# Tiles of a shared batch between the next batch's halves, gathers in front of scatters, and another order in the routing

## The chip, the cores and the metric

The kernel runs on one core of a Trainium2 chip. The metric is the device time of one execution in microseconds; the median of three runs stands for the kernel. Engines are TensorE (PE), VectorE (DVE), ScalarE (ACT), GpSimd (POOL) and SyncE (SP). SP issues the plain loads and stores, GpSimd the gathers and scatters by index; all of them run on the core's 16 DMA engines.

## The reference

Four batches of 512 tokens with 512 features pass through an attention layer and a mixture of experts, each with a residual:

```python
x = x + xattn(layernorm(x), ctx, ctx)   # keys and values: the context and the tokens, 1024 in all
x = x + ffn(layernorm(x))
# ffn, T = 2048 tokens, E = 64 experts, K = 6, CAP = 128, I = 192, SI = 384
scores = softmax(xf @ gate_w.T);  topk_w, topk_idx = top_k(scores, K)
# every expert takes its first 128 tokens in token order
gu = gx @ gate_up_proj[e];  hid = silu(gu[:, :I]) * gu[:, I:]
eo = (hid @ down_proj[e]) * buf_w            # scatter-added to the tokens
shared = (silu(xf @ shared_gate_w.T) * (xf @ shared_up_w.T)) @ shared_down_w.T
```

All is in float32. The kernel splits every operand of a product into a high and a low part and makes three matmuls of each product (high by high, high by low, low by high).

## The kernel before, in words

**First part.** A loop over the four batches does the attention and the router. The last batch (b = 3) has a body of its own, `last_routes` in the three engines' programs: the choice of experts of its tokens is not scattered to the table in HBM as for the other batches but added up with matmuls. TensorE makes the logits, then positions (`pos`), then a table of token numbers (`tab`) and one of weights (`tabw`); VectorE makes what they need (the one-hot rows `hot`, `chosen_b`, `at_slot` or `slots_hot`, `hot_w`). `idx_ready` is incremented when the rows to gather are known, `kept.routed` when the weights are too. Between these pieces lie pieces of the second part, called through `two.`.

**Second part.** Two kinds of work run together. (1) The experts, one a step: SP loads 2 x 384 KB of gate and up weights and 256 + 128 KB of down weights into rings of three raw buffers (`gu_raw`, `dn_raw`); ScalarE copies the high part (`act_weights`), VectorE subtracts the low part (`dve_weights`); GpSimd gathers 128 rows (256 KB, `gather`), TensorE transposes them (`rows`), multiplies with gate and up (`gate_up`, 12 matmuls of 384 columns), transposes the hidden tile and multiplies with down (`down`, 5 matmuls of 512 columns); ScalarE scales by the weight (`out_rows`, four buffers `eo`), and GpSimd scatters with add (`add_rows`, 256 KB). In step e TensorE does down(e), transpose_hidden(e + 1), gate_up(e + 2), rows(e + 4) and then a piece of the shared work. In step e VectorE makes the splits of experts e + 3 and e + 4; SP loads weights e + 7 when those of e + 4 are split. (2) The shared expert: each batch has three pairs (gate, up) of 12 + 12 matmuls of 512 columns, and four down tiles of 9. A half (gate or up) is spread over two steps, six matmuls in each; a down tile lies in one step, the step after it has none. The hidden tile of a pair is made by `dve_hid` and split by `act_high` and `dve_low` into one of three slots.

Scatters go in turn to two targets, `out` and `second_sum`, in the order of `SETS`; one waits for the landing of the one before it on its target. At the end one transfer adds `second_sum` to `out`.

**The order.** Batches come as 0, 3, 1, 2. Pairs 0 to 3 and the tiles (0, 0) and (0, 1) are done in the first part. `shared_events` writes the order of the rest by hand, and each engine's program of the second part follows it:

```python
for b in (0, B - 1, *range(1, B - 1)):
    for n, pair in enumerate(PAIRS):
        if pair[0] == b and n >= LEAD_PAIRS:
            events += [("gate", n), ("up", n)]
    events += [("down", tile) for tile in TILES_OF[b]]
```

So the four tiles of a batch lie behind each other in steps 12 to 18, 32 to 38 and 52 to 58, and the halves between them. GpSimd's loop over the experts is: add expert e's rows, add the rows of a shared tile if step e has one, gather for expert e + 7. Behind the routing's end SP waits for `kept.routed` before it loads expert 2's down weights, expert 4's and all that follow; x2T of the batches 1 and 2 is loaded again from HBM (2 x 1 MB each), batch 1's after pair 2, batch 2's after pair 5.

Of the kernel before, what the change touches and what calls it, by code (L numbers as in the profile page):

```python
# [25 lines left out]
ALU = mybir.AluOpType  # L26
# [3 lines left out]
P = 128  # L30
B, S, D = 4, 512, 512
T = B * S
C = D // P
# [72 lines left out]
def attention_and_router(nc, ctx, sem, t, table, x2_rows, second_sum, x2T_kept, kept):  # L106
# [322 lines left out]
    def scalar(act, two):  # L429
# [21 lines left out]
        def body(b, more):  # L451
# [32 lines left out]
            if not more:  # L484
                two.act_high(act, 0)
                two.act_silu(act, 1)
            if more:
# [14 lines left out]
            if not more:  # L502

                act.wait_ge(hot_ready, 1)
                for i in range(NT):
                    act.activation(hot_tok[:, i * K:(i + 1) * K, :], hot[:, i * K:(i + 1) * K, :], ACT.Copy,
                                   scale=value[:, i:i + 1]).then_inc(hot_tok_ready, 1)
                two.act_silu(act, 2)
                two.act_high(act, 1)
                two.act_high(act, 2)  # L510
                act.wait_ge(hot_w_made, 1)
                for n in range(2):
                    act.activation(hot_w[n][:, :, 0, :], hot[:, n * 2 * K:(n + 1) * 2 * K, :],
                                   ACT.Copy).then_inc(hot_w_high, 1)
            if more:
                h(("k", 2), ("k", 3))
# [25 lines left out]
    def vector(dve, two):  # L542
# [53 lines left out]
        def last_routes(b, after):  # L596
# [4 lines left out]
            two.dve_low(dve, 0)  # L601
            two.dve_weights(dve, 1, 2)
            low_logits = products[3][:, 0:2 * E].rearrange("p (i e) -> p i e", e=E)
# [27 lines left out]
            dve.tensor_tensor(chosen_b[:, :, :], chosen[:, :, :], third[2], ALU.add).then_inc(chosen_ready, 1)  # L631
            two.dve_hid(dve, 1)
            after(("pos", 0))
# [10 lines left out]
            for i in range(NT):  # L644
# [3 lines left out]
                                  ALU.is_equal).then_inc(slots_hot, 1)  # L648
            two.dve_low(dve, 1)

# [7 lines left out]
            dve.nop().then_inc(group_taken, 1)  # L658
            dve.nop().then_inc(kept.idx_ready, 1)  # L659
            two.dve_hid(dve, 2)  # L660
            two.dve_low(dve, 2)
# [192 lines left out]
    def tensor(pe, two):  # L854
# [53 lines left out]
        def last_routes(b):  # L908
            two.pe_gate(pe, 1)
            for n in range(2):  # L910
                claim(b, False, ("logits", n))
                for i in (2 * n, 2 * n + 1):
                    taken(b, False, ("x2T", i))
                    for c in range(C):
                        sides = gate[:, c, :, :].rearrange("p h e -> p (h e)")
                        out = bank_of(False, ("logits", n))[:, cols(i % 2, 2 * E)]
                        pe.matmul(out, x2T[0][:, c, cols(i)], sides, start=c == 0, stop=False)
                        last = pe.matmul(out, x2T[1][:, c, cols(i)], sides, start=False, stop=c == C - 1)
                last.then_inc(group_full, 1)
            two.pe_up(pe, 1)  # L920
            pe.wait_ge(chosen_ready, b + 1)
# [32 lines left out]
        def body(b, more):  # L954
# [46 lines left out]
            if not more:  # L1001
                item(b, more, "sd")
                two.pe_gate(pe, 0)
                two.pe_up(pe, 0)
            for i in range(NT):
# [76 lines left out]

def shared_events():

    events = []
    for b in (0, B - 1, *range(1, B - 1)):
        for n, pair in enumerate(PAIRS):
            if pair[0] == b and n >= LEAD_PAIRS:
                events += [("gate", n), ("up", n)]
        events += [("down", tile) for tile in TILES_OF[b]]  # L1090
    return [e for e in events if e[0] != "down" or e[1] not in TILES_OF[0][:LEAD_TILES]]


EVENT_AT, BEGUN_AT = {}, {}
for _k, _event in enumerate(shared_events()):
    EVENT_AT[2 * _k + (_event[0] != "down")] = _event
    if _event[0] != "down":
        BEGUN_AT[2 * _k] = _event
assert max(EVENT_AT) < E - 2
EVENT_STEP = {event: step for step, event in EVENT_AT.items()}  # L1100

# [18 lines left out]
def experts(nc, ctx, sem, t, table, x2_rows, second_sum, x2T_kept, kept):  # L1120
# [70 lines left out]
    def banks_before(n):  # L1191

        return max(0, n - 2) if n < LEAD_PAIRS else n - 1

# [62 lines left out]
    def gpsimd(pool):  # L1257
# [33 lines left out]
        gather(6)  # L1291
        for e in range(E):
            add_rows(("expert", e))
            if e in EVENT_AT and EVENT_AT[e][0] == "down":
                add_rows(("shared", EVENT_AT[e][1]))
            gather(e + 7)

# [29 lines left out]
    def scalar(act):  # L1327
# [21 lines left out]
        high_xgT(0)  # L1349
        out_rows(("shared", (0, 0)))  # L1350
        act.wait_ge(kept.routed, 1)
        act_weights(act, 2, 4)
        high_xgT(1)
        act_weights(act, 4, 5)
        gate(0)
        high_xgT(2)
# [7 lines left out]
        def step(e):  # L1364
            kind, n = EVENT_AT[e - 1] if e - 1 in EVENT_AT else (None, None)
            if kind == "down":
                out_rows(("shared", n))
            elif kind == "gate":
                act_silu(act, n)
            if e + 1 < E:  # L1370
                high_hidT(e + 1)
            if (kind, n) == ("down", TILES_OF[0][-1]):
                act_high(act, 3)
            out_rows(("expert", e))
            if e + 4 < E:
                act_weights(act, PIECE_NO["gu", e + 4, 0], PIECE_NO["gu", e + 4, 0] + 1)
            if e + 2 < E:
                gate(e + 2)
            if e + 4 < E:
                high_xgT(e + 4)  # L1380
            if kind == "up":
                act_high(act, n)
            if e + 4 < E:
                act_weights(act, PIECE_NO["gu", e + 4, 1], PIECE_NO["gu", e + 4, 1] + 1)
            if e + 3 < E:
                act_weights(act, PIECE_NO["dn", e + 3, 0], PIECE_NO["dn", e + 3, 0] + 1)
# [33 lines left out]
    def low_xgT(dve, e):  # L1420
        dve.wait_ge(xgT_high, e + 1)
        subtract(dve, xgT[1][:, e % 2, :], ps_xgT[:, :], xgT[0][:, e % 2, :]).then_inc(xgT_low, 1)

    def dve_prologue(dve):
        low_xgT(dve, 0)
        dve_hid(dve, 3)

    def vector(dve):
# [3 lines left out]

        def up(e):
            dve.wait_ge(silu_ready, e + 1)
            dve.tensor_tensor(hid[:, e % 2, 0:I], silu[:, e % 2, 0:I], ps_gu[:, e % 2, I:2 * I], ALU.mult)
            dve.tensor_tensor(hid[:, e % 2, I:HP], silu[:, e % 2, P:I], ps_gu[:, e % 2, I + P:2 * I],
                              ALU.mult).then_inc(hid_made, 1)

        dve_weights(dve, 2, 4)
        low_xgT(dve, 1)  # L1440
        dve_weights(dve, 4, 5)
        up(0)
        low_xgT(dve, 2)
        dve_weights(dve, 5, 7)
        up(1)
        low_xgT(dve, 3)
# [3 lines left out]
        def step(e):  # L1450
            kind, n = EVENT_AT[e - 1] if e - 1 in EVENT_AT else (None, None)
            if kind == "up":
                dve_hid(dve, n)
            if e + 3 < E:
                dve_weights(dve, PIECE_NO["gu", e + 3, 1], PIECE_NO["gu", e + 3, 1] + 1)
            if e + 2 < E:
                dve_weights(dve, PIECE_NO["dn", e + 2, 0], PIECE_NO["dn", e + 2, 0] + 1)
            if e + 1 < E:
                low_hidT(e + 1)
            if (kind, n) == ("down", TILES_OF[0][-1]):  # L1460
                dve_low(dve, 3)
            if e + 4 < E:
                dve_weights(dve, PIECE_NO["gu", e + 4, 0], PIECE_NO["gu", e + 4, 0] + 1)
            if e + 2 < E:
                up(e + 2)
            if e + 4 < E:
                low_xgT(dve, e + 4)
            if kind == "up":
                dve_low(dve, n)
        for e in range(E):  # L1470
# [37 lines left out]
    def rows(pe, e):  # L1508
# [5 lines left out]
        last.then_inc(xgT_full, 1)  # L1514

    def pe_prologue(pe):
        rows(pe, 0)
        shared_down(pe, (0, 0))

    def tensor(pe):  # L1520
        def gate_up(e):
            pe.wait_ge(xgT_low, e + 1)
            pe.wait_ge(weights_split, PIECE_NO["gu", e, 1] + 1)
            if e < 2:
                pe.wait_ge(shid_made, 3)
            else:
                pe.wait_ge(hid_made, e - 1)
            w = [h[:, :] for h in gu[e % RING]]
            for c in range(C):
                last = product(pe, ps_gu[:, e % 2, 0:2 * I], [h[:, e % 2, cols(c)] for h in xgT],  # L1530
                               [h[:, cols(c, 2 * I)] for h in w], c == 0, c == C - 1)
            last.then_inc(gu_full, 1)

        def transpose_hidden(e):
# [17 lines left out]

        rows(pe, 1)
        gate_up(0)
        rows(pe, 2)
        shared_down(pe, (0, 1))
        gate_up(1)
        rows(pe, 3)
# [3 lines left out]
        def step(e):  # L1562
# [3 lines left out]
            if e + 2 < E:  # L1566
                gate_up(e + 2)
            if e + 4 < E:
# [124 lines left out]
```

## Time and profile before

| | us |
|---|---|
| median of 3 runs | 865.02 (863.67 to 868.36) |
| profiled execution | 863.39 |
| its span in the profile | 861.7 |
| TensorE busy | 771.0 (89%) |
| VectorE busy | 596.2 (69%) |
| ScalarE busy | 452.2 (52%) |
| GpSimd busy | 317.2 (37%) |

The profiled execution's time is 1.7 above its span. Busy times are shares of a span whose parts differ: the attention until about 428, the last batch's routing until about 465, the experts until about 830, the final sum until the end. Matmul ends are modelled and pipelined, so a busy TensorE need not be at its peak.

### The profile page before, as it was taken

How to read it: one execution, taken by the hardware profiler on the slowest of the kernel's cores; microseconds unless marked ns; L12 is line 12 of the kernel's file. 1: busy time of each engine (PE TensorE's matmuls, PEld its weight loads, DVE VectorE, ACT ScalarE, POOL GpSimd, SP SyncE). 2: the span in 40 equal slices, each digit the busy share in tenths (PEclk: the TensorE clock that was granted, in tenths of full speed). 3: DMA queues.
4: the chain of work that ended last, by engine and by line, in shares of the span. 5: the costliest groups of instructions: out<-in, count | busy, mean ns of one | idle time of the engine just before them, and what ended most of it. 6: DMA issues, size and time to landing. Idle time of an engine off the chain costs nothing.

```text
span 861.7 us, 11717 instructions
## 1 busy us (share of the span) xinstructions
PE 771.0 (89%) x3862; PEld 651.7 (76%) x3862; DVE 596.2 (69%) x1168; ACT 452.2 (52%) x798; POOL 317.2 (37%) x256
## 2 busy tenths in 40 slices
PE   4999999899998999899988999998999989999930
PEld 3888877678776787788877888887887977888720
DVE  6427567565685655864686989787899877998820
ACT  4333323233333423243344888786888877888820
POOL 1001010652107520074104556456544656555640
PEclk9999999999999999999999999999999999999985
DMA  6842262321622227212827999999999999999968
GB/s 233 288 158 80 79 233 98 100 98 61 257 72 99 98 74 268 97 38 77 308 83 240 283 317 321 339 321 315 315 314 319 311 313 318 315 314 298 249 91 177
DMA packets 69158, 180.31 MB, mean 209 GB/s; under 512 B 10144, under 2 KB 10528, under 8 KB 64416
## 3 DMA queue, kind: packets, MB, share of 16 engines
q1 hardware_dynamic: 49632, 137.65, 46.2%
q0 software_dynamic: 19472, 42.02, 22.0%
q8 instruction: 24, 0.39, 0.2%
q14 instruction: 30, 0.25, 0.1%
HBM read 143.33 MB, written 44.97 MB: 219 GB/s over the span
## 4 chain that ended last, share of the span: by engine, by line
PE 53%; DMA 13%; DVE 12%; issue 10%; POOL 5%; ACT 3%; SPq 1%; DVEq 0%; ACTq 0%; POOLq 0%
PE bank L1066 8%; PE bank L1067 8%; PE bank L1068 8%; DMA xg<-x_rows,idx_all 5%; DMA stage<-wvT_in 3%; PE ps_gu L1066 3%; PE ps_gu L1068 3%; PE ps_gu L1067 3%; DMA second_sum<-product,idx_all 2%; PE ps_xgT L1513 2%; POOL second_sum L1276 2%; POOL out_rows L1276 2%; PE scores L1066 2%; PE ps_sh L1068 2%; PE ps_sh L1066 2%
## 5 line engine op out<-in xcount | busy, mean ns | idle before, releaser
L1392 DVE TENSOR_TENSOR gu_lo<-gu_raw,gu_hi 128x768 fp32r<-128x768 f32 x128 | 122.1, 956 | 24.5 <-ACT gu_hi L1309 23.4
L413 POOL DMA_INDIRECT table<-rows,slot x72 | 81.5, 1132 | 137.3 <-DVEq L822 116.5
L1309 ACT ACTIVATE gu_hi<-gu_raw 128x768 fp32r<-128x768 f32 x128 | 107.2, 840 | 11.6 <-PE bank L1068 8.9
L1268 POOL DMA_INDIRECT xg<-x_rows,idx_all x64 | 74.9, 1171 | 53.1 <-DVEq L659 28.6
L1066 PE MATMUL ps_gu<-gu_hi,xgT_hi 128*128 128x384 f32 x256 | 92.2, 360 | 0.0
L1068 PE MATMUL ps_gu<-gu_hi,xgT_lo 128*128 128x384 f32 x256 | 86.9, 339 | 0.0
L1067 PE MATMUL ps_gu<-gu_lo,xgT_hi 128*128 128x384 f32 x256 | 86.7, 339 | 0.0
L442 ACT ACTIVATE qT_hi<-bank 128x512 fp32r<-128x512 f32 x32 | 19.2, 599 | 116.3 <-PE bank L1068 116.3
L447 ACT ACTIVATE pbuf<-scores,negmax 128x1024 f32<-128x1024 f32 x16 | 17.9, 1117 | 85.4 <-DVE negmax L593 85.4
L1066 PE MATMUL bank<-xnT_hi,w_hi 128*128 128x512 f32 x128 | 51.1, 399 | 2.8 <-DVE xnT_lo L571 2.8
L571 DVE TENSOR_TENSOR qT_lo<-bank,qT_hi 128x512 fp32r<-128x512 f32 x32 | 22.0, 689 | 44.2 <-ACT qT_hi L442 44.2
L1513 PE MATMUL ps_xgT<-ident,xg 128*128 128x128 f32 x256 | 39.2, 275 | 14.3 <-DMA xg<-x_rows,idx_all 12.6
L1067 PE MATMUL bank<-xnT_lo,w_hi 128*128 128x512 f32 x128 | 50.6, 395 | 0.0
L1068 PE MATMUL bank<-xnT_hi,w_lo 128*128 128x512 f32 x128 | 50.5, 395 | 0.0
L1392 DVE TENSOR_TENSOR xgT_lo<-ps_xgT,xgT_hi 128x512 fp32r<-128x512 f32 x64 | 43.9, 687 | 9.0 <-ACT xgT_hi L1330 7.3
L1276 POOL DMA_INDIRECT second_sum<-product,idx_all x20 | 34.0, 1698 | 43.9 <-ACT product L1346 27.6
L1067 PEld LDWEIGHTS ps_gu<-gu_lo,xgT_hi 128*128 128x128 f32 x256 | 49.1, 192 | 0.0
L1066 PEld LDWEIGHTS ps_gu<-gu_hi,xgT_hi 128*128 128x128 f32 x256 | 49.0, 191 | 0.0
L1068 PEld LDWEIGHTS ps_gu<-gu_hi,xgT_lo 128*128 128x128 f32 x256 | 48.6, 190 | 0.0
L1392 DVE TENSOR_TENSOR dn_lo<-dn_raw,dn_hi 128x512 fp32r<-128x512 f32 x64 | 44.1, 690 | 6.2 <-ACT dn_hi L1315 3.3
L1276 POOL DMA_INDIRECT second_sum<-eo,idx_all x20 | 33.2, 1662 | 40.4 <-DMA second_sum<-product,idx_all 23.6
L1330 ACT ACTIVATE xgT_hi<-ps_xgT 128x512 fp32r<-128x512 f32 x64 | 38.1, 596 | 15.3 <-PE ps_xgT L1513 11.0
(257 smaller groups left out, 2209.6 us busy)
## 6 DMA issues: line engine op xcount, KB each, us to landing
gu_raw<-gate_up_in SPq DMA_DIRECT2D x128, 384.0 KB, 9.9
dn_raw<-down_in SPq DMA_DIRECT2D x64, 256.0 KB, 6.2
dn_raw<-down_in SPq DMA_DIRECT2D x64, 128.0 KB, 10.0
x_rows<-pbuf SPq DMA_DIRECT2D x17, 256.0 KB, 2.1
stage<-wqT_in SPq DMA_DIRECT2D x4, 1024.0 KB, 4.8
stage<-wkT_in SPq DMA_DIRECT2D x4, 1024.0 KB, 4.8
stage<-ctxT_in SPq DMA_DIRECT2D x4, 1024.0 KB, 5.5
stage<-wvT_in SPq DMA_DIRECT2D x4, 1024.0 KB, 8.9
```

The lines of the kernel that those rows point to most:

```text
L413: pool.indirect_dma_start(out=table, out_offset=bass.IndirectOffsetOnAxis(ap=slot[:, i, k:k + 1], axis=0), in_=rows[:, i, k, :], in_offset ...
L442: act.activation(split_dest(group)[0], split_source(key, group), ACT.Copy).then_inc(high_done, 1)
L571: dve.tensor_tensor(lo, split_source(key, group), hi.bitcast(F32), ALU.subtract).then_inc(group_taken, 1)
L1066: pe.matmul(out, still[0], moving[0], start=first, stop=False)
L1067: pe.matmul(out, still[0], moving[1], start=False, stop=False)
L1068: return pe.matmul(out, still[1], moving[0], start=False, stop=last)
L1268: pool.indirect_dma_start(out=xg[:, e % 3, :], out_offset=None, in_=x2_rows, in_offset=index(("expert", e))).then_inc(gathered[e % 3], 16)
L1276: pool.indirect_dma_start(out=(t["out"], second_sum)[r % 2], out_offset=index(what), in_=eo[r % EO], in_offset=None, compute_op=ALU.add).t ...
L1309: act.activation(gu[n % RING][0][:, half(part)], gu_raw[:, n % RING, half(part)], ACT.Copy).then_inc(weights_high, 1)
L1330: act.activation(xgT[0][:, e % 2, :], ps_xgT[:, :], ACT.Copy).then_inc(xgT_high, 1)
L1392: return dve.tensor_tensor(lo, x, hi.bitcast(F32), ALU.subtract)
L1513: last = pe.transpose(ps_xgT[:, cols(c)], xg[:, e % 3, cols(c)], ident[:, :])
```

## The change

The order of the shared work is another one: the tiles of a batch alternate with the halves of the next batch (half, tile, half, tile, ...), as long as there are tiles; the last batch's four tiles stay together at the end (steps 52 to 58). Since the next batch's pairs are now made while tiles of the batch before still need the slots, `SPLITS` says behind which event a pair's hidden tile is split. GpSimd gathers for expert e + 7 before it adds the rows of expert e. In the routing the first up half goes behind the transposes of x2, gate 1 behind the logits, VectorE's split of expert 0's second piece, hidden tile 1 and its split move back; expert 0's gate and up product, expert 1's transposed rows and the split of expert 1's gate and up weights move ahead of the table of weights and thus of `kept.routed`. A gate half waits for the hidden tile of the pair before it.

```diff
@@ scalar, last batch
             if not more:
                 two.act_high(act, 0)
-                two.act_silu(act, 1)
...
+                two.act_silu(act, 1)
                 two.act_silu(act, 2)
                 two.act_high(act, 1)
                 two.act_high(act, 2)
...
+                act.wait_ge(kept.idx_ready, 1)
+                two.act_weights(act, 2, 4)
@@ vector, last_routes
             two.dve_low(dve, 0)
-            two.dve_weights(dve, 1, 2)
...
             dve.tensor_tensor(chosen_b[:, :, :], chosen[:, :, :], third[2], ALU.add).then_inc(chosen_ready, 1)
-            two.dve_hid(dve, 1)
+            two.dve_weights(dve, 1, 2)
...
                                   ALU.is_equal).then_inc(slots_hot, 1)
-            two.dve_low(dve, 1)
+            two.dve_hid(dve, 1)
...
             dve.nop().then_inc(kept.idx_ready, 1)
+            two.dve_low(dve, 1)
             two.dve_hid(dve, 2)
@@ tensor, last_routes
         def last_routes(b):
-            two.pe_gate(pe, 1)
+            two.pe_up(pe, 0)
             for n in range(2):
...
                 last.then_inc(group_full, 1)
+            two.pe_gate(pe, 1)
             two.pe_up(pe, 1)
@@ tensor, body
                 two.pe_gate(pe, 0)
-                two.pe_up(pe, 0)
             for i in range(NT):
@@ the order
+def shared_events(batches):
+    order, tiles = [], list(TILES_OF[0][LEAD_TILES:])
+    for b in batches:
+        halves = [(side, n) for n, pair in enumerate(PAIRS) if pair[0] == b and n >= LEAD_PAIRS
+                  for side in ("gate", "up")]
+        while tiles:
+            order += [halves.pop(0), ("down", tiles.pop(0))]
+        order += halves
+        tiles = list(TILES_OF[b])
+    return order + [("down", tile) for tile in tiles]
+EVENTS = shared_events((B - 1, *range(1, B - 1)))
...
+SPLITS = {}
+_at = 0
+for _n in range(LEAD_PAIRS - 1, len(PAIRS)):
+    _before = PAIRS[(_n // 3 - 1) * 3][0]
+    _at = max(_at + 1, EVENTS.index(("down", TILES_OF[_before][-1])))
+    if ("up", _n) in EVENTS:
+        _at = max(_at, EVENTS.index(("up", _n)))
+    SPLITS[EVENTS[_at]] = _n
...
-        return max(0, n - 2) if n < LEAD_PAIRS else n - 1
+        return max(0, n - 1) if n < LEAD_PAIRS else n
@@ gpsimd
         for e in range(E):
+            gather(e + 7)
             add_rows(("expert", e))
             if e in EVENT_AT and EVENT_AT[e][0] == "down":
                 add_rows(("shared", EVENT_AT[e][1]))
-            gather(e + 7)
@@ scalar, second part
         out_rows(("shared", (0, 0)))
+        gate(0)
+        high_xgT(1)
         act.wait_ge(kept.routed, 1)
-        act_weights(act, 2, 4)
-        high_xgT(1)
         act_weights(act, 4, 5)
-        gate(0)
...
-            if (kind, n) == ("down", TILES_OF[0][-1]):
-                act_high(act, 3)
...
-            if kind == "up":
-                act_high(act, n)
+            if (kind, n) in SPLITS:
+                act_high(act, SPLITS[kind, n])
@@ vector, second part
     def dve_prologue(dve):
         low_xgT(dve, 0)
         dve_hid(dve, 3)
+        dve_weights(dve, 2, 4)
+        up(dve, 0)
+        low_xgT(dve, 1)
...
-            if kind == "up":
-                dve_low(dve, n)
+            if (kind, n) in SPLITS:
+                dve_low(dve, SPLITS[kind, n])
@@ tensor, second part
     def pe_prologue(pe):
         rows(pe, 0)
         shared_down(pe, (0, 0))
+        gate_up(pe, 0)
+        rows(pe, 1)
 
     def tensor(pe):
...
-        rows(pe, 1)
-        gate_up(0)
         rows(pe, 2)
         shared_down(pe, (0, 1))
-        gate_up(1)
+        gate_up(pe, 1)
```

## Rows read from the trace of the kernel before

**Rows 1.** The page: its first line, and the busy tenths of the DMA engines in 40 slices.

```profile
span 861.7 us, 11717 instructions
...
DMA  6842262321622227212827999999999999999968
```

**Rows 2.** TensorE's waits: who waited for whom, us in total, times, longest.

```profile
PE ps_xgT L1513 <- DMA xg<-x_rows,idx_all: 12.6, 9, 2.3
...
PE ps_dn L1066 <- DVE pT_lo L1392: 6.1, 3, 2.0
```

**Rows 3.** Timeline of TensorE, line 1551, seven of 64: start, us, instruction.

```profile
477.95 0.63 PE L1551 MATMUL ps_dn<-dn_hi,hidT_lo 128*128 128x512 f32 x1
...
556.82 0.40 PE L1551 MATMUL ps_dn<-dn_hi,hidT_lo 128*128 128x512 f32 x1
...
562.80 0.40 PE L1551 MATMUL ps_dn<-dn_hi,hidT_lo 128*128 128x512 f32 x1
...
566.71 0.39 PE L1551 MATMUL ps_dn<-dn_hi,hidT_lo 128*128 128x512 f32 x1
...
611.88 0.40 PE L1551 MATMUL ps_dn<-dn_hi,hidT_lo 128*128 128x512 f32 x1
...
617.16 0.40 PE L1551 MATMUL ps_dn<-dn_hi,hidT_lo 128*128 128x512 f32 x1
...
772.50 0.40 PE L1551 MATMUL ps_dn<-dn_hi,hidT_lo 128*128 128x512 f32 x1
```

**Rows 4.** Windows of the experts: us, busy PE, PEld, DVE, ACT, POOL, PEclk, DMA share, GB/s.

```profile
543.00:607.00 64.00, 56.56 (x283) 49.06 (x281) 49.10 (x85) 46.30 (x87) 34.49 (x24) 0.92 1.06 324
607.00:659.00 52.00, 52.00 (x288) 46.70 (x287) 47.38 (x82) 44.89 (x83) 27.86 (x22) 1.00 1.06 314
660.00:720.00 60.00, 52.71 (x278) 45.88 (x277) 48.63 (x84) 45.95 (x86) 34.47 (x23) 0.97 1.06 312
720.00:772.00 52.00, 52.00 (x288) 46.70 (x287) 47.33 (x82) 44.78 (x83) 28.28 (x22) 1.00 1.07 316
772.00:805.00 33.00, 30.37 (x167) 26.89 (x167) 28.16 (x49) 26.53 (x51) 18.34 (x12) 1.00 1.05 302
```

**Rows 5.** DMA queues in the window 720 to 772: packets, MB, share of 16 engines.

```profile
q1 hardware_dynamic: 4682, 10.82, 63.0%
q0 software_dynamic: 2379, 5.56, 43.3%
```

**Rows 6.** Tile gu_raw: its loads issued in 720:730, 740:750 and 760:770.

```profile
DMA to landing us min/median/max: 6.9/7.1/7.5
...
DMA to landing us min/median/max: 8.0/8.7/9.2
...
DMA to landing us min/median/max: 10.3/10.4/10.7
```

**Rows 7.** Timeline of GpSimd and, at 630.26, of TensorE.

```profile
630.10 1.57 POOL L1276 DMA_INDIRECT out_rows<-eo,idx_all  x1 [2.40 <-ACT eo L1346]
630.26 0.60 PE L1513 MATMUL ps_xgT<-ident,xg 128*128 128x128 f32 x4
631.97 1.02 POOL L1268 DMA_INDIRECT xg<-x_rows,idx_all  x1 [0.31 <-issue]
...
697.74 2.12 POOL L1276 DMA_INDIRECT out_rows<-product,idx_all  x1 [0.62 <-DMA out_rows<-eo,idx_all]
706.33 1.85 POOL L1276 DMA_INDIRECT out_rows<-eo,idx_all  x1 [2.17 <-DMA out_rows<-product,idx_all]
...
829.91 1.56 POOL L1276 DMA_INDIRECT second_sum<-eo,idx_all  x1 [0.90 <-DMA second_sum<-product,idx_all]
```

**Rows 8.** Timelines in the routing: TensorE, GpSimd, VectorE.

```profile
442.42 0.20 PE L925 MATMUL bank<-earlier,ones 128*128 128x64 bf16 x1 [3.53 <-DVE chosen_b L631]
...
454.53 1.03 POOL L1268 DMA_INDIRECT xg<-x_rows,idx_all  x1 [28.55 <-DVEq L659]
...
465.17 0.23 DVE L679 TENSOR_TENSOR tab<-bank,product 128x64 f32<-128x64 f32 x1
```

More of the change, by code:

```diff
@@ L1080 @@
 TILES_OF = {b: [(b, i) for i in range(NT)] for b in range(B)}
[L1083 to L1091, printed above, removed]
+def shared_events(batches):
[9 more added lines that the diff above has]
+EVENTS = shared_events((B - 1, *range(1, B - 1)))
 EVENT_AT, BEGUN_AT = {}, {}
-for _k, _event in enumerate(shared_events()):
+for _k, _event in enumerate(EVENTS):
     EVENT_AT[2 * _k + (_event[0] != "down")] = _event
@@ L1422, in low_xgT, with up @@
         subtract(dve, xgT[1][:, e % 2, :], ps_xgT[:, :], xgT[0][:, e % 2, :]).then_inc(xgT_low, 1)
+    def up(dve, e):
+        dve.wait_ge(silu_ready, e + 1)
+        dve.tensor_tensor(hid[:, e % 2, 0:I], silu[:, e % 2, 0:I], ps_gu[:, e % 2, I:2 * I], ALU.mult)
+        dve.tensor_tensor(hid[:, e % 2, I:HP], silu[:, e % 2, P:I], ps_gu[:, e % 2, I + P:2 * I],
+                          ALU.mult).then_inc(hid_made, 1)
     def dve_prologue(dve):
@@ L1431, in low_hidT @@
             subtract(dve, hidT[1][:, e % 2, :], ps_hidT[:, 0:HP], hidT[0][:, e % 2, :]).then_inc(hidT_low, 1)
[L1433 to L1440, printed above, removed]
         dve_weights(dve, 4, 5)
-        up(0)
         low_xgT(dve, 2)
         dve_weights(dve, 5, 7)
-        up(1)
+        up(dve, 1)
         low_xgT(dve, 3)
@@ L1459, in step @@
                 low_hidT(e + 1)
-            if (kind, n) == ("down", TILES_OF[0][-1]):
-                dve_low(dve, 3)
             if e + 4 < E:
@@ L1464, in step @@
             if e + 2 < E:
-                up(e + 2)
+                up(dve, e + 2)
             if e + 4 < E:
                 low_xgT(dve, e + 4)
-            if kind == "up":
-                dve_low(dve, n)
+            if (kind, n) in SPLITS:
+                dve_low(dve, SPLITS[kind, n])
         for e in range(E):
@@ L1514, in rows, with gate_up @@
         last.then_inc(xgT_full, 1)
+    def gate_up(pe, e):
+        pe.wait_ge(xgT_low, e + 1)
+        pe.wait_ge(weights_split, PIECE_NO["gu", e, 1] + 1)
+        if e < 2:
+            pe.wait_ge(shid_made, 3)
+        else:
+            pe.wait_ge(hid_made, e - 1)
+        w = [h[:, :] for h in gu[e % RING]]
+        for c in range(C):
+            last = product(pe, ps_gu[:, e % 2, 0:2 * I], [h[:, e % 2, cols(c)] for h in xgT],
+                           [h[:, cols(c, 2 * I)] for h in w], c == 0, c == C - 1)
+        last.then_inc(gu_full, 1)
     def pe_prologue(pe):
@@ L1518, in pe_prologue @@
         shared_down(pe, (0, 0))
+        gate_up(pe, 0)
+        rows(pe, 1)
     def tensor(pe):
[L1521 to L1532, printed above, removed]
         def transpose_hidden(e):
@@ L1566, in step @@
             if e + 2 < E:
-                gate_up(e + 2)
+                gate_up(pe, e + 2)
             if e + 4 < E:
```

## The prediction

> **What bounds the kernel now.** Times are us from the span's start; d(e) is the start of expert e's last down matmul (L1551), which marks the steps.
>
> I read the page first: the span and how full the DMA engines are in each slice [rows 1]. From the 23rd of its 40 slices on, where the expert loop begins, the DMA row shows nines almost to the end. Then the waits of TensorE: its largest is for the gathered rows, and three waits of 2.0 are for the low half of the shared hidden tile, at the first down tile of a batch [rows 2].
>
> The steps come next [rows 3]. A step with half of a gate or up product takes 617.16 - 611.88 = 5.28. A step with a shared down tile takes 5.98 and the bare one after it 3.91 (556.82, 562.80, 566.71). The difference of 1.37 for six 512-column matmuls makes 0.23 each. Steps 0 to 51 hold 32 half steps and, ten times, a down step and a bare one: 32 x 5.28 + 10 x 9.89 = 267.9. They took 772.50 - 477.95 = 294.5, so 26.6 is stall or slow clock. It all lies around the bunches of down tiles: between them TensorE is busy 52.00 of 52.00, in them 56.56 of 64 and 52.71 of 60, at a granted clock of 0.92 and 0.97 [rows 4].
>
> Why do the bunches stall? Two steps of a bunch carry three scatters. Each scatter waits for the one before it on its target (out or the second sum): 697.74 to 706.33 is 8.6, with two targets 4.3 per scatter [rows 7]. Three take 12.9 where the steps take 9.89, and a gather stands behind them on GpSimd's queue.
>
> The last reading decides the forecast. DMA moved 314, 312 and 316 GB/s in windows of very different work [rows 4], share 1.06 or 1.07 each time. An expert needs 1.18 MB of weights, 0.262 gathered and 0.262 scattered, 1.704 MB: in 5.28 that is 323 GB/s. In 720 to 772 TensorE kept its pace but the weight queue delivered 10.82 MB [rows 5], 208 GB/s, where 1.18 MB per 5.28 is 223. The shortfall, 0.8 MB, shows as later landings: 7.1, 8.7, 10.4 [rows 6]. So the DMA engines are already short by some 2% in the half steps; the stalls of the bunches let them catch up. I take 316 GB/s for what they can do with this mix.
>
> **The change part by part.**
> *Alternating tiles and halves.* Same matmuls, same scatters. Ten of the down tiles now lie between halves, so that four steps (5.28 + 5.28 + 5.98 + 3.91 = 20.45) hold five scatters. The scatter targets allow five per 21.5: nearly even, and the stretches of pure halves give the rest back. The shared hidden tile is split well ahead of its first down tile for batches 3 and 1, so two of the three 2.0 waits go; the one at d(52), where the last four tiles stay bunched, remains. At TensorE's pace all 26.6 except some 4 for leftover scatter lag would go. But the four steps need 4 x 1.704 + 0.262 = 7.08 MB, 346 GB/s; at 316 they take 22.4. For steps 0 to 51: 52 x 1.704 + 10 x 0.262 + 2.1 for one batch's x2T = 93.3 MB, 295 us at 316, what they take today. The alternation removes stalls that DMA then takes back.
> What is left is threefold. (a) A load is issued three steps before its split, 15.3, and lands after 10.4 [rows 6]; starved, TensorE can run one expert closer to its data: 1.18 MB / 316 = 3.7. (b) DMA ran under 316 where it was waiting for stalled engines: 312 in 60 us and 302 in 33 [rows 4], 0.8 + 1.5 = 2.3. (c) the routing, below.
> A page gives another result: the Trainium skill, "DMA: Bandwidth & Descriptors", Specifications, puts the HBM limit of one core near 358 GB/s. By it 346 would fit and the alternation would keep TensorE's pace, which is the first rival below; no window of these rows reaches it.
> *VectorE* has 47.33 of 52 busy in half steps [rows 4], 4.81 a step with 0.35 of shared work in it. Four alternating steps need 4 x 4.46 + 0.69 = 18.5 of 20.45: no bound. The later splits move 0.6 to 0.7 each and wait behind nothing.
> *Gather in front of the scatter.* In a pure half step, d(26) = 611.88 + 3 x 5.28 = 627.72: the scatter issues at 630.10, the gather behind it at 631.97, while the transposes that free its buffer end at 630.86 [rows 7]. Now the scatter waits for them and the gather's issue: 630.86 + 0.3 + 1.02 + 0.3 = 632.5, 2.4 late. Cover: a target is used every 10.56 and its cycle is 8.6, so 2.0 is free, and four eo buffers stand before ScalarE stalls. Without cover it costs up to 2.4 per scatter. The gather itself is earlier by a whole scatter with its wait, so the gather waits [rows 2] should go. I price the swap at nothing; bounds 0 and rival three.
> *Stricter waits for the banks* (`banks_before`). A gate half now waits until the hidden tile of the pair before is made. The up half ends a step and VectorE makes the tile first thing in the next (0.69), while TensorE still has the down, the transpose and the gate and up product of experts ahead of the gate half, some 3. In the routing, gate 3 waits for hidden tile 1, made right behind the slots, before the table's matmuls end. Both at nothing; if the cover went, 0.7 each.
> *Routing.* The first up half (12 x 0.23 = 2.8) moves behind the x2T transposes and gate 1 behind the logits, so choosing the experts begins about 2.6 sooner. Gate and up 1 (5.5) fit into the gap that follows, where TensorE idles 3.53 waiting for the choice [rows 8]. On VectorE the split that moved behind the choice costs 0.96 against 0.69 for the product it replaces; the rest moves behind the slots or the indices. The first gather goes from 454.53 [rows 8] to about 452.1. Then expert 0's gate and up product and a transpose (12 x 0.17 + 0.35 = 2.4) and ScalarE's two weight copies go ahead of the weights' table, so `routed`, after 465.40 (465.17 + 0.23 [rows 8]), moves to about 466.5. Before it, ScalarE has the new wait for `idx_ready`, passed some 5 before ScalarE comes to it; behind it stand the two copies (1.6), the silu of pair 3 and expert 0's first copy of its transposed rows, which come out about level with today. VectorE's sum of the weights' table is queued behind a split of 1.8, expert 0's product and a low part. SP's loads of expert 2's down weights and everything later are queued behind it, 1 late, though buffers are then already free and the loads follow without gaps. Less is left for TensorE behind `routed`: I get d(0) about 2.5 sooner. The estimate is built from these moves; bounds 0 (it stays with SP) and 4. For the DMA-bound sum I take 2.0.
>
> Sum: 3.7 + 2.3 + 2.0 = 8.0. From d(52) on nothing is reordered except the gathers: the last scatter is issued 829.91 - 772.50 = 57.4 later [rows 3, 7], then come its landing and the final sum, as now. The profiled execution took 863.4 (span 861.7 and 1.7 around it); 855.4 after. The median of the runs, 865.0, lies 1.6 higher: 857.
>
> **The rivals.**
> 1. DMA can do more when asked. For it: 324 GB/s in 543 to 607, with the x2T load in it [rows 4]. Against: the growing landings [rows 6] while nothing else held the queue. Then 26.6 - 4 + 2.5 = 25 comes off: 840. Chance 0.20.
> 2. Only the routing's gain, or not even that, arrives: DMA takes back everything, since starving ScalarE, in order, also holds its silu and transposes behind the weight copies, and the last bunch unchanged. 861 to 865. Chance 0.17.
> 3. Slower: the scatter, now behind the gather's wait, makes the scatter chain the bound. The 62 scatters of steps 0 to 51 have 294.5 + 2.5 = 297; the point is 4.8 per scatter, 9.6 per target cycle against 8.6 now. With the full 2.4 added the cycle is 11.0, 62 x 5.5 = 341, the worst end, +44; half of it (9.8) gives 304, +7: 872. Against: when GpSimd is behind, the transposes have long been done and the wait costs nothing, so that the delay and a full cycle hardly meet. Chance 0.07.
>
> **The numbers.** The forecast itself has 0.56, its own range 852 to 862 (316 GB/s give or take 2% would be 6; the head 0 to 4). Half a per cent, 4.3, is about what a measurement of this kernel can tell from no change. Nearly all of the forecast case and rival 1 are below 860.7: faster 0.74. Same 0.18, from rival 2 and the forecast's edge. Slower 0.08. Range 842 to 863: half of rival 1 and part of rival 2 inside.
>
> **What would show it.** Right: DMA share stays at 1.06 and near 316 GB/s through steps 0 to 51, landings of gate_up weights at 12 to 15, ScalarE waiting for gu_raw or dn_raw, no TensorE wait for gathered rows or, before d(52), for the hidden tile's low half; first gather near 452, `routed` near 466.5, d(0) near 475.5, d(52) near 764. Wrong: 340 GB/s or more in the alternating steps with TensorE full (rival 1), or scatters of one target more than 9.6 apart with ScalarE waiting for them (rival 3).

## The result, and the profile after

The changed kernel takes 863.1 us (median of 20 runs), the kernel before 865.8 (20 runs beside them); all times below are in us; the ratio is 0.9959, 95% interval 0.9943 to 0.9976. On another chip it was 0.9981 (0.9964 to 0.9997, e9 below). Forecast were 857 and a range of 842 to 863. The change is faster, but by 3.5 (0.41%) where 8.0 were forecast, and just outside the range.

Where did it go? The profile has a span of 861.3. The expert loop, by the same line of `down` (L1560 now), start of its matmul for experts 0, 52 and 53:

```profile
474.71 0.39 PE L1560 MATMUL ps_dn<-dn_hi,hidT_lo 128*128 128x512 f32 x1
...
767.75 0.39 PE L1560 MATMUL ps_dn<-dn_hi,hidT_lo 128*128 128x512 f32 x1
...
780.47 0.44 PE L1560 MATMUL ps_dn<-dn_hi,hidT_lo 128*128 128x512 f32 x1
```

| | d(0) | d(52) | d(53) | d(63) | end |
|---|---|---|---|---|---|
| before | 477.95 | 772.50 | 780.76 | 827.41 | 861.7 |
| after | 474.71 | 767.75 | 780.47 | 826.51 | 861.3 |
| gained | 3.2 | 4.8 | 0.3 | 0.9 | 0.4 |

So 3.2 are there at the first expert, where the routing is done, another 1.5 come in steps 0 to 51, and 4.5 are lost again inside one step. (The two spans are nearly alike; this execution took 863.1 and that of before 863.4, while the medians are 2.8 apart, so the last column understates the gain. The first shared gate matmul, ahead of which nothing was changed, starts at 422.44 before and 423.31 after, 0.9 later. Counted from it, d(0) comes 4.1 sooner and d(52) 5.6.)

The routing, in timelines of TensorE, GpSimd and VectorE, against [rows 8]:

```profile
440.79 0.20 PE L928 MATMUL bank<-earlier,ones 128*128 128x64 bf16 x1 [0.82 <-DVE chosen_b L632]
...
452.23 1.03 POOL L1280 DMA_INDIRECT xg<-x_rows,idx_all  x1 [25.39 <-DVEq L660]
...
466.82 0.23 DVE L681 TENSOR_TENSOR tab<-bank,product 128x64 f32<-128x64 f32 x1
```

TensorE waits 0.82 for the choice of experts instead of 3.53, the first gather goes 2.3 earlier, and `routed` comes after 467.05 instead of 465.40, 1.65 later.

Steps 0 to 51 as one window, before and after (us, busy PE, PEld, DVE, ACT, POOL, granted clock, DMA share, GB/s):

```profile
478.00:772.50 294.50, 278.26 (x1479) 246.04 (x1478) 252.83 (x434) 238.21 (x444) 163.65 (x114) 0.97 1.06 317
```

```profile
474.70:767.80 293.10, 277.34 (x1480) 239.51 (x1478) 246.95 (x432) 233.43 (x443) 163.06 (x114) 0.99 1.06 318
```

And who waited, after, from step 0 to 51 (us in total, times, longest):

```profile
ACT dn_hi L1326 <- DMA dn_raw<-down_in: 42.4, 38, 2.3
...
ACT gu_hi L1321 <- DMA gu_raw<-gate_up_in: 9.4, 10, 6.1
```

The loads of gate and up weights issued in 740 to 750, against [rows 6]:

```profile
DMA to landing us min/median/max: 13.2/13.7/14.2
```

TensorE's waits for gathered rows [rows 2] are gone from the list, and so are those for the hidden tile's low half, but for one. In their place ScalarE waits 42.4 for down weights and 9.4 for gate and up weights, landings are at 13.7 where they were 8.7 in the same stretch, and the rate is 318 GB/s against 317. The same bytes went through at the same rate, only another engine now waits for them.

The step that gives it back, after, in timelines of ScalarE, VectorE and TensorE:

```profile
769.21 0.63 ACT L1326 ACTIVATE dn_hi<-dn_raw 128x512 fp32r<-128x512 f32 x1 [1.14 <-DMA dn_raw<-down_in]
...
772.52 0.62 ACT L1337 ACTIVATE pT_hi<-shid 128x512 fp32r<-128x512 f32 x1
```

```profile
768.45 0.68 DVE L1421 TENSOR_TENSOR shid<-ssilu,ps_sh 128x512 f32<-128x512 f32 x1
...
774.02 0.68 DVE L1401 TENSOR_TENSOR pT_lo<-shid,pT_hi 128x512 fp32r<-128x512 f32 x1
```

```profile
774.76 0.79 PE L1068 MATMUL ps_dn<-xnT_hi,pT_hi 128*128 128x512 f32 x1 [3.79 <-DVE pT_lo L1401]
```

The same matmul before:

```profile
777.67 0.50 PE L1066 MATMUL ps_dn<-xnT_hi,pT_hi 128*128 128x512 f32 x1 [2.03 <-DVE pT_lo L1392]
```

Windows after:

```profile
767.00:775.00 8.00, 4.21 (x24) 3.54 (x24) 7.56 (x15) 6.01 (x12) 4.68 (x4) 0.92 1.06 308
775.00:781.00 6.00, 6.00 (x17) 4.65 (x18) 1.95 (x3) 1.44 (x3) 0.66 (x1) 0.54 1.04 319
```

VectorE has the last pair's hidden tile at 769.13. ScalarE's copy of it (L1337) comes only at 772.52: it stands behind a down weight copy that waited for its load (769.21), two more weight copies and the rest of the step. The low half is ready at 774.70, TensorE idles 3.79 before the tile at 774.76, and then runs at a granted clock of 0.54 until 781, near the lower of its two levels (1.2 GHz): 512-column matmuls start every 0.43 instead of every 0.23. Before, the same wait was 2.0 [rows 2], the step 8.3 long, and the clock stayed up (1.00 in 772 to 805 [rows 4]); now it is 12.7 long: 1.8 more of waiting and 2.7 more of slow matmuls.

### The profile page after: what moved, and what is told of

It reads as the page before. It is cut to its first block, busy times and chain, and to the rows that moved or that the text cites. A ratio compares the mean times of both kernels' runs of the same rounds, so it can differ in the third digit from the quotient of the medians.

```text
span 861.3 us, 11718 instructions
## 1 busy us (share of the span) xinstructions
PE 774.3 (90%) x3862; PEld 649.2 (75%) x3862; DVE 591.3 (69%) x1168; ACT 447.7 (52%) x798; POOL 316.5 (37%) x256
## 4 chain that ended last, share of the span: by engine, by line
PE 39%; DMA 29%; DVE 13%; issue 8%; ACT 4%; POOL 2%; SPq 1%; DVEq 0%; ACTq 0%; POOLq 0%
DMA dn_raw<-down_in 11%; PE bank L1068 8%; PE bank L1069 8%; PE bank L1070 8%; DMA out_rows<-product,idx_all 5%; DMA stage<-wvT_in 3%; DMA out_rows<-eo,idx_all 3%; DMA gu_raw<-gate_up_in 2%; DMA second_sum<-eo,idx_all 2%; PE scores L1068 2%; DVE xn L810 2%; PE scores L1070 2%; PE scores L1069 2%; DMA second_sum<-product,idx_all 2%; PE bank L897 2%
## 5 line engine op out<-in xcount | busy, mean ns | idle before, releaser
L1326 ACT ACTIVATE dn_hi<-dn_raw 128x512 fp32r<-128x512 f32 x64 | 40.3, 630 | 47.3 <-DMA dn_raw<-down_in 44.4
L402 POOL TENSOR_TENSOR rstd<-veps,half 128x1 f32<-128x1 f32 x16 | 11.9, 745 | 88.8 <-DVE veps L743 88.8
L1401 DVE TENSOR_TENSOR dn_hi<-dn_raw,dn_hi 64x512 fp32r<-64x512 f32 x64 | 43.9, 686 | 0.9
## 6 DMA issues: line engine op xcount, KB each, us to landing
gu_raw<-gate_up_in SPq DMA_DIRECT2D x128, 384.0 KB, 13.7
```

The source lines that it names most:

```text
L1326: act.activation(hi[:, 0:D], raw[:, 0:D], ACT.Copy)
L1401: return dve.tensor_tensor(lo, x, hi.bitcast(F32), ALU.subtract)
```

## The experiments

They ran on three other chips (e1 to e4, e5 to e8 and e9 to e12 on one each), on which the kernel before takes 906.5, 907.4 and 907.4. There the attention, ahead of everything changed here, takes 40 to 46 longer; the changed kernel's loop is alike on both (e9). The kernel before has a profile on the first chip alone. To be free of the attention, the table counts from the first matmul of the shared gate (422.44 in before). "52 to 53" is the length of step 52. Ratios are to before on the same chip; the other columns come from one profile each.

| | ratio (95%) | to d(0) | d(0) to d(52) | 52 to 53 | d(53) to end |
|---|---|---|---|---|---|
| before (first chip) | 1 | 55.5 | 294.5 | 8.3 | 80.9 |
| after (first chip) | 0.9959 (0.9943, 0.9976) | 51.4 | 293.0 | 12.7 | 80.8 |
| e1 order only | 0.9962 (0.9938, 0.9986) | 55.0 | 293.7 | 11.8 | 80.9 |
| e2 gather only | 0.9976 (0.9946, 1.0006) | 55.1 | 290.6 | 9.7 | 80.4 |
| e3 after, fewer bytes | 0.9664 (0.9619, 0.9710) | 51.0 | 272.4 | 8.3 | 78.1 |
| e4 before, fewer bytes | 0.9830 (0.9786, 0.9875) | 53.6 | 284.7 | 8.3 | 78.8 |
| e5 routing only | 0.9971 (0.9948, 0.9994) | 50.9 | 298.6 | 9.7 | 78.6 |
| e6 after, early split | 0.9949 (0.9926, 0.9971) | 51.0 | 291.5 | 8.6 | 82.8 |
| e7 after, early load | 0.9977 (0.9952, 1.0002) | 51.0 | 293.2 | 9.8 | 81.3 |
| e8 after, x2T in two | 0.9973 (0.9946, 1.0000) | 51.0 | 291.6 | 11.2 | 80.9 |
| e9 after again | 0.9981 (0.9964, 0.9997) | 51.0 | 292.9 | 12.9 | 80.2 |
| e10 e6 and e7 | 0.9943 (0.9925, 0.9961) | 50.9 | 293.1 | 9.9 | 82.3 |
| e11 e10, tiles later | 0.9943 (0.9920, 0.9965) | 51.0 | 291.2 | 7.7 | 86.2 |
| e12 after, old gather | 0.9971 (0.9952, 0.9989) | 51.0 | 292.1 | 10.0 | 81.7 |

**Is it bandwidth? e3 and e4.** A quarter of the gate and up bytes of experts 3 to 63 is left out:

```diff
-            sp.dma_start(gu_raw[:, n % RING, half(part)], t["gate_up"][n][:, half(part)]
+            some = half(part) if n < RING else slice(part * GU // 2, part * GU // 2 + GU * 3 // 8)
+            sp.dma_start(gu_raw[:, n % RING, some], t["gate_up"][n][:, some]
                          ).then_inc(gu_loaded[n % RING][part], 16)
```

The matmuls use what an earlier expert left in the buffer. e3, in the changed kernel: 

> The changed kernel with a quarter of the gate and up weights from expert 3 on not loaded (288 KB instead of 384 KB a piece; the matmuls use what an earlier expert left there, all else runs as it did): 1.507 MB an expert instead of 1.704. Theory A: alternating steps then need 6.29 MB in 20.45, 308 GB/s, under 316, so TensorE keeps its pace: d(52) - d(0) 270 to 276 instead of 293, ScalarE's waits for weights nearly gone, ratio to before about 0.975. Theory C (weights are late because SP issues them late or their latency is fixed, not for lack of bandwidth): landings stay at 13 to 15 and d(52) - d(0) above 288.

e4, in the kernel before: 

> The kernel before with the same quarter of the gate and up weights from expert 3 on not loaded. Theory A: half steps stay at 5.28, the bunches stay bound by the scatter chain and the gathers behind it, so d(52) - d(0) falls only to 284 to 290 from 294.5; it is then 12 to 18 us above the changed kernel with the same loads left out, which is what the alternation is worth where DMA has room. Theory C: no difference to before beyond 2 us.

The loops came out as theory A has it: 272.4 (270 to 276 expected) and 284.7 (284 to 290); e3's ratio, 0.9664, is lower than the 0.975 expected. Windows of e3 and of e4, in e4 a bunch of tiles and the halves behind it:

```profile
660.00:720.00 60.00, 60.00 (x332) 53.86 (x331) 56.45 (x98) 53.53 (x101) 38.49 (x27) 1.00 1.06 304
720.00:786.00 66.00, 66.00 (x367) 59.33 (x366) 61.10 (x108) 58.40 (x111) 42.08 (x29) 1.00 1.07 307
```

```profile
583.00:640.00 57.00, 50.65 (x268) 44.08 (x267) 46.37 (x81) 44.64 (x84) 35.16 (x23) 0.98 1.06 311
640.00:697.00 57.00, 56.58 (x311) 50.55 (x310) 52.07 (x90) 47.98 (x89) 28.80 (x23) 0.99 1.02 285
```

In e4 the bunch still costs TensorE 6.4 of 57, while behind it the rate falls to 285 GB/s with TensorE busy 56.58 of 57: nothing more is asked for.

In e3 TensorE is busy 60.00 of 60 and 66.00 of 66 through tiles and halves alike; ScalarE's waits for down weights in steps 0 to 51, 42.4 in the changed kernel, are

```profile
ACT dn_hi L1327 <- DMA dn_raw<-down_in: 0.5, 2, 0.3
```

With the smaller bytes in both, the change is worth 284.7 - 272.4 = 12.3 in the loop, with all bytes 294.5 - 293.0 = 1.5. (It is the whole change; how much of the 12.3 is the order's and how much the gather's, no run separates.) Theory C, a fixed latency or late issues, falls: issues, buffers and waits are the same, only the bytes are fewer, and the waits are gone. Landing times, its other sign, are not in these two traces. Note the share: it is 1.06 and 1.07 in e3, where hardly anybody waits for a load. A full share does not say that DMA is the bound; landings that grow, and whose wait ends on a load, do.

**Which part does it? e1, e2, e5, e12.** Each is one part of the change alone in the kernel before (e12: all but the gather's swap).

```diff
# e2; e12 is the changed kernel with this undone
         for e in range(E):
+            gather(e + 7)
             add_rows(("expert", e))
             if e in EVENT_AT and EVENT_AT[e][0] == "down":
                 add_rows(("shared", EVENT_AT[e][1]))
-            gather(e + 7)
# e1: shared_events(batches), SPLITS and the wait below, nothing of the routing or of GpSimd
-        return max(0, n - 2) if n < LEAD_PAIRS else n - 1
+        return max(0, n - 2) if n < LEAD_PAIRS else n
# e5: the hunks of last_routes, of the prologues and of the start of the second part
```

e1: 

> Before with the order of the shared work alone changed: tiles between halves, splits as in SPLITS, gathers behind the scatters and the routing as before. Theory A (the DMA engines at 316 GB/s bound steps 0 to 51, a late split at step 52 gives the rest back): d(0) stays at 478, d(52) - d(0) about 291 to 294 as in both kernels (294.5 and 293.0), ScalarE waits some 40 us for down weights, a long wait of 3 to 4 at the tile of step 52; ratio 0.998 to 1.004. Theory B (the order is good for 20 us, and the gather put in front of the scatters spoils it): d(52) - d(0) about 272 and ratio 0.975.

e2: 

> Before with the gather in front of the scatter alone. Theory A: the waits of TensorE for gathered rows (12.6 in before) vanish, but the scatter chain still holds the bunches through the eo buffers and DMA bounds the rest: 0 to 4 us less, ratio 0.995 to 1.000. Theory B: each scatter is 2.4 us later, ratio 1.005 or more.

e5: 

> Before with the routing's part of the change alone, old order of the shared work, gathers behind the scatters. Theory A (DMA at its limit through steps 0 to 51, the end set by the scatters of the last bunch): the loads are not sooner, but the stalls in the bunches are those of the scatters, so d(0) is 3 sooner and most of it stays at d(52), d(52) - d(0) 293 to 296; ratio 0.996 to 0.999. Rival: DMA takes it back by d(52), which is then where it was, ratio 0.999 to 1.002.

e12: 

> The changed kernel with the gather behind the scatters, as before. Theory A: where the weights are late, neither the gathers nor the scatters are what TensorE waits for: d(52) - d(0) 291 to 295, ratio within 0.003 of the changed kernel's. Rival F (the swap is what carries the gain): gathers late again, TensorE waits 5 or more for them, ratio 0.999 or more.

The order alone leaves the loop at 293.7 with a step 52 of 11.8: theory B falls. Its ratio is below 1 by 0.4% all the same, under the 0.998 to 1.004 that was expected, and ScalarE waits 24.7 for down weights where some 40 were. Its profiled execution took 906.9 where its median is 904.5, and from gate 0 to the end it is 2.2 longer than before, so the profile cannot say where the 0.4% come from. The gather alone takes 4.0 off the loop (290.6), its ratio's interval includes 1. The routing alone brings d(0) 4.1 sooner (50.9 against 55.0 and 55.1 in e1 and e2), and the loop takes 4.1 back (298.6 against 294.5): the rival's reading of d(52), not mine, though the ratio is within mine. In e12 only 3.5 of waits for gathered rows return (5 or more for rival F), and the loop is 292.1 against 292.9 in e9: where the weights are late, the swap changes nothing that can be seen. Each part alone, and order and routing together (e12), has a ratio of 0.996 to 0.998, with intervals too wide to tell them apart. Nor do the profiles, one each, share the gain out: from gate 0 to d(52) the order alone gains 1.3, the gather alone 4.4 and the routing alone 0.5, in sum 6.2, the whole 5.6 (e9: 6.1), but order and routing without the gather 7.0.

**What gives it back? e6, e10, e11.** e6 splits the last pair in front of step 52's scaling and its gate and up weight copies; the down copies of the step before stay ahead of it:

```diff
             if e + 1 < E:
                 high_hidT(e + 1)
+            if (kind, n) == ("up", len(PAIRS) - 1):
+                act_high(act, n)
             out_rows(("expert", e))
...
-            if (kind, n) in SPLITS:
+            if (kind, n) in SPLITS and SPLITS[kind, n] != len(PAIRS) - 1:
                 act_high(act, SPLITS[kind, n])
# and the same with dve_low behind low_hidT
```

> The changed kernel with the last pair's hidden tile split in front of the weight copies of step 52 instead of behind them. Theory A: step 52 is 6 to 8 long instead of 12.7, with a wait under 1 instead of 3.8 and no fall of the clock behind it; the tail follows, 3 to 5 us less than the changed kernel, ratio to before 0.990 to 0.993. Rival D (the tail is bound by the chain of scatters whatever TensorE does): d(53) is 4 to 6 sooner, d(63) - d(53) longer by the same, ratio as the changed kernel's, 0.996.

```profile
811.07 0.50 PE L1068 MATMUL ps_dn<-xnT_hi,pT_hi 128*128 128x512 f32 x1 [2.31 <-DVE pT_lo L1403]
```

```profile
805.00:814.00 9.00, 6.69 (x36) 5.72 (x35) 7.72 (x15) 6.48 (x12) 4.48 (x3) 1.00 1.08 318
```

The wait is 2.31, not under 1: a down copy ahead of the split still waits 1.21 for its load (until 807.38). The clock stays at 1.00 and the step takes 8.6 instead of the 12.9 of e9. Of these 4.3 the stretch from d(53) to the end takes 2.6 back (82.8 against 80.2). Between A and D, then; the ratio is 0.9949 against 0.9981 (e9) and 0.9959 of the changed kernel on two other chips, with intervals that overlap.

Of the 4.3 the shorter wait makes 2.1 (4.4 in e9, 2.3 here). The rest is the clock's, and the split does not settle it. Step 52 in all profiles with all bytes, by TensorE's wait in it, and how much longer TensorE was busy there than the 6.23 of before:

| | before | e2 | e5 | e10 | e6 | e12 | e7 | e8 | after | e1 | e9 |
|---|---|---|---|---|---|---|---|---|---|---|---|
| wait | 2.0 | 2.0 | 2.0 | 2.0 | 2.3 | 2.3 | 3.3 | 3.6 | 3.8 | 4.1 | 4.4 |
| busy longer | 0 | 1.4 | 1.4 | 1.6 | 0.0 | 1.5 | 0.2 | 1.4 | 2.7 | 1.5 | 2.2 |

e2 has the old order, the old split and the old wait, and loses 1.4 to the clock all the same; e10 has e6's split and loses 1.6:

```profile
815.61 0.50 PE L1066 MATMUL ps_dn<-xnT_hi,pT_hi 128*128 128x512 f32 x1 [2.03 <-DVE pT_lo L1392]
```

e7 loads expert 4's weights ahead of the wait for `routed`, e8 spreads batch 2's x2T, e10 is e6 and e7 together, e11 also moves the last tiles:

```diff
# e7
+        load_gu(sp, 4)
         sp.wait_ge(kept.routed, 1)
         load_dn(sp, 2)
-        load_gu(sp, 4)
# e8
-            if e == EVENT_STEP["up", 5] + 1:
+            if e == EVENT_STEP["up", 5] + 3:
                 sp.wait_ge(sup_full, 6)
-                load_x2T(sp, 2)
+                load_x2T(sp, 2, (0,))
+            if e == EVENT_STEP["up", 5] + 11:
+                load_x2T(sp, 2, (1,))
# e11
-    EVENT_AT[2 * _k + (_event[0] != "down")] = _event
+    _late = _event[0] == "down" and _event[1] in TILES_OF[B - 2]
+    EVENT_AT[2 * _k + (_event[0] != "down" or _late)] = _event
```

e7: 

> The changed kernel with expert 4's gate and up weights loaded as soon as their buffer is split, ahead of SP's wait for the routing's end (786 KB some 3 us sooner, at a time when the DMA engines are idle). Theory A: bytes moved into idle time count in full: 0.786 MB / 316 = 2.5 at most, d(52) 1.5 to 2.5 sooner against d(0). Theory C (weights late for another reason than bandwidth): d(52) - d(0) stays at 293.

e8: 

> The changed kernel with batch 2's x2T (2 x 1 MB) loaded in two parts, at steps 14 and 22, instead of both at step 12. Theory A: the same bytes: the stall of 6.3 at step 16 shrinks or splits in two, but other steps take it over, d(52) - d(0) within 2 of 293. Rival E (the burst itself costs, by stopping the copies behind it): d(52) - d(0) 5 to 6 less.

e9: 

> The changed kernel itself, so that the other experiments stand beside it on one chip. From the first shared matmul (gate 0, L1068) to the end of the span it took 438.0 in its first profile, before 439.3. Expected here 436 to 439, ratio to before 0.995 to 0.997.

e10: 

> The changed kernel with both the early split of the last pair (as in e6) and the early load of expert 4's gate and up weights (as in e7). If the two gains add: gate 0 to the end 431 to 434 (e6 alone 433.8, e7 alone 435.2), ratio to before 0.991 to 0.994. If the early load is taken back by the bunch at the end: as e6, 0.995.

e11: 

> As e10, and the last four tiles in steps 53, 55, 57, 59 instead of 52, 54, 56, 58, so that the first finds its split done. Theory A: no wait of TensorE for the hidden tile's low half and no fall of the clock behind it, steps 52 and 53 together 10 instead of 12.4 or more; 1 to 3 less than e10, ratio 0.988 to 0.993. Rival D (the chain of scatters holds the end): the tiles' scatters come one step later, so the end is that of e10 or up to 2 later.

e7 missed: d(0) to d(52) is 293.2, as without it. What was moved is 0.786 MB, 2.5 at the most, and none of it is seen. Its trace shows that expert 4's load went 5.6 sooner, but expert 5's is issued 47.7 after gate 0 as in e9, when its buffer is free. The bytes did move (20.02 MB in the first 80 after gate 0 against 19.56 in e9, 104.41 against 103.84 up to d(52)); why TensorE is no further is open, and this result alone speaks for theory C. e8 is as A has it. The stall in the changed kernel, at step 16, behind the x2T load, ScalarE and TensorE:

```profile
563.74 0.84 ACT L1321 ACTIVATE gu_hi<-gu_raw 128x768 fp32r<-128x768 f32 x1 [6.11 <-DMA gu_raw<-gate_up_in]
```

```profile
566.02 0.69 PE L1548 MATMUL ps_hidT<-ident,hid 128*128 128x128 f32 x2 [6.34 <-DVE hid L1436]
```

splits in e8 into idle times of 2.75 in step 18 and 2.39 in step 26, and the loop is 291.6, within 2. e9's ratio is nearer to 1 than was expected, its length from gate 0 (436.9) as expected. e10 does not add the two gains (436.2 from gate 0). e11 missed by theory A: TensorE still idles 3.3 in step 52 though no tile stands there, and steps 52 and 53 take 15.1 where 10 were expected (13.8 in e10). It waits for its expert's own hidden tile, whose split stands behind a down copy that waited for its load (811.71): the late weights stop TensorE with or without the tile. From d(52) to the end it takes 7.7 + 86.2 = 93.9 against 9.9 + 82.3 = 92.2 in e10, the length that rival D has; the ratio is e10's. e10 and e11, at 0.9943, are the fastest with all bytes; e10's interval lies below that of the changed kernel on its chip only just (0.9961 against 0.9964).

## Why the prediction was wrong

**Right:** the bound. "I take 316 GB/s" against 318 measured; the loop's 26.6 of stalls was not to be had, as forecast, and e3 and e4 show why. Landings were forecast at 12 to 15 and are 13.7; ScalarE waits for loads; no waits for gathered rows; the first gather near 452 (452.23), `routed` near 466.5 (467.05), d(0) near 475.5 (474.71). Rival 1 (840) falls with the 318 GB/s. Rival 3 falls because no wait of ScalarE for a scatter is listed in steps 0 to 51 after, though scatters of one target are at times 10 to 15 apart; it waits for weights, and TensorE for tiles that stand behind these waits.

By the figure of the Trainium skill, "DMA: Bandwidth & Descriptors", Specifications (near 358 GB/s from HBM for one core), the 346 of the alternating steps would have fitted. The runs do not reach it with this mix of loads, gathers and adding scatters: 315 to 322 over steps 0 to 51 in every kernel with all its bytes.

**Where it failed, first:** "From d(52) on nothing is reordered". True of the order, not of the time: step 52 took 12.7 instead of 8.3. The split of the last pair had always stood behind the weight copies in ScalarE's queue. That cost 2.0 while the copies found their data, and the prediction kept it at that. My own forecast said that ScalarE would wait for loads, and I did not ask what was queued behind those waits where a tile follows at once. The waits added 1.8, and the clock at 0.54 another 2.7, a term that the prediction did not have. The latter is in large part chance, as the table of step 52 shows: with the old split and its wait of 2.0 it is 0 in before and 1.4 in e2 and e5. e6 shows that an earlier split shortens the wait (2.3), e11 that late loads stop TensorE in this step even without a tile. e6 gets 4.3 back in the step, of which 1.7 are left at the end.

**Second:** term (b) of the sum 3.7 + 2.3 + 2.0. It counts 2.3 for windows under 316 GB/s, but before already ran at 317 over steps 0 to 51 (324 in 543 to 607 [rows 4]), so there was nothing to catch up, and 1.5 of it was read in 772 to 805, behind d(52). The bytes from gate 0 on, in MB, show the terms apart:

| | first 80 | first 344 | up to d(52) | d(52) after gate 0 |
|---|---|---|---|---|
| before | 18.43 | 102.40 | 104.33 | 350.1 |
| after | 19.25 | 103.25 | 103.36 | 344.4 |
| e9, after again | 19.56 | 103.86 | 103.84 | 343.9 |
| e5, routing only | 19.62 | 102.53 | 104.38 | 349.6 |

Up to 344 the changed kernel had moved 0.85 MB more, 2.7 at 318 GB/s, of it 0.82 MB in the first 80, behind the new routing: term (c), forecast 2.0. (`routed` comes later, but the loads of expert 5's gate and up weights, which wait for their buffer, go out at 471.46 instead of 474.11.) At d(52) it had moved 0.97 MB less for the same work, 3.1: TensorE runs that much closer to its data, term (a), forecast 3.7. For (b) nothing is left. So 5.6 of the 8.0 came up to d(52), counted from gate 0, and 4.8 from the span's start. e9, on another chip, makes 3.6, 1.5 and 1.0 of (c), (a) and (b), so the terms by themselves are known only roughly. In e5 the head's lead is there too, and is gone at 344; it was lost in the loop with the old bunches, where the rate fell to 287 between 240 and 280 after gate 0. That is no proof that DMA at its limit took it back.

**Third:** the tail. Coming sooner to d(53) makes the stretch behind it longer (e6 +2.6, e10 +2.1 against e9), as rival D has it in part. In e6 the chain that ended last goes over a down weight load of 13.1 (issued at 821.51) and then from scatter to scatter; no run tests which of them holds the end. Rival 2 of the prediction, 861 to 865, has the right size by luck: it lets DMA take back everything but the routing's gain, and up to d(52) that is not what happened.

Open: why e1 is faster than its profile, why e7's earlier bytes do not show, and what sets the clock behind a wait. Nor was it tried what the limit of 315 to 322 GB/s consists of: bytes, packets, or the adding scatters in the mix. These rates differ by 2%, 6 in the loop, which is more than any part of the change; the gather alone, in the old order, had 290.6, less than the 293.0 of the whole.

## What to carry to other kernels

Before stalls are smoothed away, multiply out the bytes behind the stretch: if the rate in the undisturbed steps is already the rate of the whole, smoothing only moves the wait to another engine. When a change makes an engine wait for loads, look at what stands behind these waits in its queue, at the next place where somebody needs it at once. Time won ahead of a stretch bound by DMA counts by the bytes that have moved by then, and a lead that is used up counts once: compare bytes at a fixed time and bytes at the same step. And a window below the limit is room only if the whole stretch is below it.

## What the runs showed of the hardware

The DMA share read 1.06 to 1.07 both where loads were late (after, 318 GB/s) and where hardly any engine waited for one (e3, 307 GB/s). After a wait of TensorE of 2.0 the granted clock was 1.00 in step 52 of before and 0.66 (548 to 553) after the same wait at 548.20; after 3.79 it was 0.54 for 6 us, after 3.3 in e7 1.00 (the step lost 0.2). The length of the wait alone does not tell. One chip ran the kernel before at 866, three others at 906.5 to 907.4; the difference lies ahead of the expert loop, where the changed kernel had a granted clock of 0.98 in 100 to 300 on the first and 0.93 on one of the others (e9).
